# A two-block transformer kernel: a norm moved to ScalarE, two rows made by TensorE, a final norm by halves, and new instruction orders

## The reference

```
x = x + norm(attn(norm(x)))
x = x + norm(ffn(norm(x)))

attn(x):                       # g, b: gain and shift of the affine norm ln
    n  = ln(x, g, b)
    W1, W2 = mlp_h1(n), mlp_h2(n)          # 128 -> 512 -> 128, exact Gelu
    t  = ln(gelu(tril(W1 W2^T) n), g, b)
    return x + mlp_fm(ln(x + t, g, b))     # 128 -> 512 -> 128

ffn(x):                        # ternary weights, one scale per output
    h = silu(x w1 s1) * (x w2 s2)          # 128 -> 512
    h = gelu(h h1 s);  h = gelu(h h2 s)    # 512 -> 512, twice
    return h w3 s3                         # 512 -> 128
```

## Time and profile before

| | |
|---|---|
| time, median of 3 runs | 376.3 us (376.24 to 377.04) |
| profiled execution | 377.94 us |
| its span, first to last instruction | 376.1 us, mean granted TensorE clock 0.991 |
| busy, share of the span | TensorE 95%, VectorE 89%, ScalarE 79%, GpSimd 31% |
| instructions | TensorE 1751 matmuls, VectorE 978, ScalarE 515, GpSimd 186 |
| moved by transfers | 9.27 MB, most of it in the first 36 us |

### The profile page before, as it was taken

How to read it: one execution, slowest core, us unless ns; L and a number is a source line. 1 busy time by engine, 2 the same in 40 slices (tenths; PEclk the granted TensorE clock), 3 DMA queues, 4 the chain that set the end, 5 groups by cost and what they waited for, 6 DMA issues and landing times.

```text
span 376.1 us, 5883 instructions
## 1 busy us (share of the span) xinstructions
PE 358.6 (95%) x1751; PEld 289.8 (77%) x1751; DVE 333.4 (89%) x978; ACT 298.4 (79%) x515; POOL 116.8 (31%) x186
## 2 busy tenths in 40 slices
PE   7889999989999999999999999999999999999891
PEld 6658788867888788878788878788787877778681
DVE  5899999999999987999899988888978989987735
ACT  4798899787679796998688779897798769878670
POOL 5520312641182017421832083034600352061111
PEclk9899999999999999999999999999999999999998
DMA  7761000000000000100000000000000100000001
GB/s 235 227 204 57 0 2 1 3 0 0 3 0 0 2 1 0 30 0 3 0 30 0 2 15 14 0 2 29 2 2 0 30 1 0 1 27 3 0 30 31
DMA packets 8545, 9.27 MB, mean 25 GB/s; under 512 B 576, under 2 KB 6336, under 8 KB 8512
## 3 DMA queue, kind: packets, MB, share of 16 engines
q1 hardware_dynamic: 7968, 8.60, 7.5%
q10 hardware_dynamic: 544, 0.26, 0.2%
HBM read 6.77 MB, written 2.10 MB: 24 GB/s over the span
## 4 chain that ended last, share of the span: by engine, by line
PE 84%; DVE 9%; ACT 3%; issue 2%; DMA 1%; POOL 0%; POOLq 0%; SPq 0%; DVEq 0%; ACTq 0%
PE bank L1144 9%; PE bank L1142 8%; PE bank L1177 7%; PE bank L1178 7%; PE bank L1026 6%; PE bank L1030 6%; PE bank L1045 6%; PE bank L1042 6%; PE bank L1027 5%; PE bank L1043 5%; PE bank L1069 4%; PE bank L972 4%; PE bank L1125 4%; PE bank L1128 3%; PE bank L1056 3%
## 5 line engine op out<-in xcount | busy, mean ns | idle before, releaser
L434 ACT ACTIVATE h_hidden_hi<-bank,cols 128x512 fp32r<-128x512 f32 x64 | 43.1, 706 | 14.6 <-PE bank L1030 13.4
L635 DVE TENSOR_TENSOR ffn_gate_lo<-bank,ffn_gate_hi 128x512 fp32r<-128x512 f32 x64 | 42.5, 684 | 6.4 <-ACT bank L504 5.4
L635 DVE TENSOR_TENSOR h_hidden_lo<-bank,h_hidden_hi 128x512 fp32r<-128x512 f32 x64 | 42.1, 678 | 2.9 <-ACT bank L439 2.6
L504 ACT ACTIVATE bank<-bank,cols 128x512 f32<-128x512 f32 x64 | 41.4, 671 | 0.7
L439 ACT ACTIVATE bank<-bank,cols 128x512 f32<-128x512 f32 x64 | 41.4, 679 | 0.1
L1142 PE MATMUL bank<-ffn_gate_hi,ffn_w_hi 128*128 128x512 f32 x92 | 37.3, 406 | 0.8 <-ACT ffn_gate_hi L489 0.8
L1144 PE MATMUL bank<-ffn_gate_lo,ffn_w_hi 128*128 128x512 f32 x92 | 36.3, 395 | 0.4 <-DVE ffn_gate_lo L635 0.4
L301 POOL TENSOR_SCALAR ln_f_ve<-ln_f_mv 128x4 f32<-128x4 f32 x8 | 1.8, 227 | 94.9 <-DVE ln_f_mv L625 94.9
L1026 PE MATMUL bank<-aT_hi,attn_w_lo 128*128 128x512 f32 x64 | 26.6, 415 | 0.9 <-DVE attn_w_lo L635 0.6
L498 ACT ACTIVATE ffn_gate_hi<-bank,cols 128x512 fp32r<-128x512 f32 x32 | 21.5, 697 | 7.3 <-PE bank L1144 4.6
L498 ACT ACTIVATE ffn_h_hi<-bank,cols 128x512 fp32r<-128x512 f32 x32 | 21.6, 701 | 7.1 <-PE bank L1144 4.7
(11 more groups left out here) (163 smaller groups left out, 1111.5 us busy)
## 6 DMA issues: line engine op xcount, KB each, us to landing
raw<-ffn_w SPq DMA_DIRECT2D x5, 512.0 KB, 3.7
out<-X SPq DMA_DIRECT2D x7, 256.0 KB, 2.3
raw<-attn_w SPq DMA_DIRECT2D x6, 256.0 KB, 5.0
X<-x SPq DMA_DIRECT2D x2, 256.0 KB, 5.5
raw<-ffn_w SPq DMA_DIRECT2D x1, 256.0 KB, 4.0
bc<-rows SPq DMA_DIRECT2D x1, 192.0 KB, 4.1
X<-x SPq DMA_DIRECT2D x1, 128.0 KB, 2.4
X<-x ACTq DMA_DIRECT2D x1, 128.0 KB, 2.7
```

Source lines behind the costliest of these rows:

```text
L434: nc.scalar.activation(dst, bank(f"{L}u{j}", c)[:, :], ACT.Gelu, bias=bias_of(L, j)).then_inc(*hi[L].done(c, j))
L635: return nc.vector.tensor_tensor(dst, whole, high.bitcast(f32), ALU.subtract)
```

## The change

1. `y_norm(0)`, `y_norm(1)` and `y_norm(2)` leave VectorE. ScalarE gets `y_normalise(c)` for these chunks, and `y_r(c)` on GpSimd computes two more values for every chunk, -mean times r.
2. `bc` is no longer loaded. TensorE transposes the columns g and b, each broadcast over 128 columns (`make_rows`), and ScalarE copies the result to `bc` (`rows_out`). fm's second bias is loaded as one row of 512 bytes. `cols` takes the second place in SyncE's queue. `fill` makes 6 and 14 transposes instead of 26 and 3.
3. The last norm goes by halves of two tiles, each with its transposes (into two PSUM banks), statistics, aggregate, power, centring and sum.
4. `TURNS` and the orders of all five lists are new. On VectorE `gate_constants` moves from behind `attn_w_lo(1)` to the second place and `n_second(0)` from before the weight halves to behind `attn_w_lo(2)`; on ScalarE `nT_high(0)` moves from behind `attn_w_hi(1)` to behind `attn_w_hi(5)`, and `ffn_w_hi(0)` ahead of `up_hi("h1", 0, 0)`; on TensorE two `up_mm` of chunk 1 stand ahead of the scores of chunk 0.

```diff
-            sp.dma_start(bc[:, :, :], rows.rearrange("(o r) d -> o r d", o=1).broadcast_to([P, 3, D])).then_inc(rows_in, 16)
+            sp.dma_start(cols[:, :], columns).then_inc(cols_in, 16)
             attn_piece(0)
-            sp.dma_start(cols[:, :], columns).then_inc(cols_in, 16)
             attn_piece(1)
             attn_piece(2)
+            sp.dma_start(b2_row[:, :], rows[2:3, :]).then_inc(b2_in, 16)
...
             def y_r(c):
+                if c:
+                    pool.wait_ge(*y.at(c - 1))
                 rstd(y_rstd, "y", y_stats, c)
+                pool.wait_ge(*y_rstd.at(c, 1))
+                nc.gpsimd.tensor_tensor(y_mr[:, :], mv("y")[:, :, 0], LN["y"]["r"][:, :], ALU.mult).then_inc(*y_rstd.done(c, 2))
+                pool.wait_ge(*y_rstd.at(c, 2))
+                nc.gpsimd.tensor_tensor(y_shift[:, :], zeros[:, :], y_mr[:, :], ALU.subtract).then_inc(*y_rstd.done(c, 3))
...
+            def last_rstd(k):
+                pool.wait_ge(*last_ve.at(0, k))
+                half = slice(2 * k, 2 * k + 2)
+                nc.gpsimd.tensor_tensor(LN["f"]["r"][:, half], LN["f"]["ve"][:, half], neg_half[:, half], ALU.pow).then_inc(*last_r.done(0, k))
...
+            def rows_out():
+                act.wait_ge(*rows_made.at(0))
+                nc.scalar.activation(flat(bc[:, :, :]), bank("rb", 0)[:, 0:2 * P], ACT.Copy).then_inc(*rows_ready.done(0))
...
+            def y_normalise(c):
+                if c:
+                    act.wait_ge(*yT_.at(c - 1))
+                else:
+                    act.wait_ge(*ffn_lo.at(0, FP - 1))
+                act.wait_ge(*y_rstd.at(c, 3))
+                for t in range(T):
+                    last = nc.scalar.activation(YF[:, t, :], X[:, c * T + t, :], ACT.Identity,
+                                                scale=LN["y"]["r"][:, t:t + 1], bias=y_shift[:, t:t + 1])
+                last.then_inc(*y.done(c))
...
-            attn_w_hi(0); attn_w_hi(1); n_high(0); nT_high(0); attn_w_hi(2); attn_w_hi(3); up_hi("h1", 0, 0); up_hi("h1", 1, 0)
+            rows_out(); attn_w_hi(0); attn_w_hi(1); attn_w_hi(2); attn_w_hi(3); attn_w_hi(4); n_high(0); attn_w_hi(5)
+            nT_high(0); ffn_w_hi(0); up_hi("h1", 0, 0); up_hi("h1", 1, 0); up_act("h1", 0, 0); up_act("h1", 1, 0); ffn_w_hi(1)
...
-            x_st(0); x_ag(0); n_first(0); n_second(0); attn_w_lo(0); attn_w_lo(1); gate_constants(); nT_low(0); x_st(1)
+            x_st(0); gate_constants(); x_ag(0); n_first(0); attn_w_lo(0); attn_w_lo(1); attn_w_lo(2); n_second(0); attn_w_lo(3)
+            x_st(1); x_ag(1); nT_low(0); attn_w_lo(4); ffn_w_lo(0); attn_w_lo(5); up_lo("h1", 0, 0); up_lo("h1", 1, 0)
+            n_first(1); ffn_w_lo(1); up_lo("h1", 2, 0); up_lo("h1", 3, 0); n_second(1); fm_bias_add(); x_st(2)
...
+            layer_lo("b", 3, 7); last_evict_second(); last_stats(0); last_aggregate(0); last_stats(1); last_centre(0)
+            last_aggregate(1); last_sum(0); last_centre(1); last_sum(1)
...
+            def make_rows():
+
+                bank_free("rb", 0)
+                pe.wait_ge(cols_in, 16)
+                for r, col in ((R_G, C_G), (R_B, C_B)):
+                    last = nc.tensor.transpose(bank("rb", 0)[:, r * P:(r + 1) * P], cols[:, col:col + 1].broadcast_to([P, P]), ident[:, :])
+                last.then_inc(*rows_made.done(0))
...
-            fill("nT", 0, 26); n_transpose(0); fill("h1u0", 0, 3); up_mm("h1", 0, 0); up_mm("h1", 1, 0); up_mm("h1", 2, 0)
+            fill("rb", 0, 6); make_rows(); fill("nT", 0, 14); n_transpose(0); up_mm("h1", 0, 0); up_mm("h1", 1, 0)
...
+            up_mm("h1", 0, 1); up_mm("h1", 1, 1); lo_sum(2); scores(0, 0); scores(1, 0); up_mm("h2", 0, 1); up_mm("h2", 1, 1)
```

596 lines of the change are left out of this document (302 added, 294 removed), and 44 rows, old and new, of the table TURNS.

## The result

The changed kernel took 379.58 us (median of 4 runs, 379.31 to 379.71) where the kernel before took 376.27 us (375.98 to 377.04): ratio 1.0084, 95% interval 1.0066 to 1.0101. It is slower by 0.8%; 373.9 us had been forecast, and the time lies outside the range given. Its profiled execution has a span of 377.8 us, against 376.1 us. Two executions of the kernel before among those that the experiments add (403.3 and 381.9 us) were in a slower state of the chip, and are left out throughout.

A forecast was written before the change was run, and what follows sets the result against it. TensorE alone bounds the long middle, TensorE and VectorE 46.3 to 100.6 us; gains lie before 100 us and in the tail. Start -1.4, feed-forward norm -0.7, middle 0, end 0, tail -0.25: -2.35 us, giving 373.9 us, range 371.2 to 376.5 us.

The forecast's parts named there:

- rival 1: Middle: ScalarE's queue is not covered, the norm costs 2 x 1.5 us and chunk 0 gives nothing; 377.65 us, chance 0.15.
- The base: Sum: -2.35 us, worked out on the profiled execution (377.94 us), was taken off the runs' median of 376.3 us.
- step (c): Start: weights land earlier, but nT_high(0) stands behind all six pieces; third matmul at 11.6 us, 0.7 us later.
- Rival 2: Start: loads at 254, not 352 GB/s; sixth piece 1.65 us later, VectorE's lead becomes +0.2 us; 375.5 us, chance 0.10.
- step (e): Start: nine fill transposes fewer on TensorE, which ran while it waited, cost nothing and save nothing.
- (a): Start: without the bc load and with cols second in the queue, n_first(0) starts at 4.8 us, 0.55 us earlier.
- (b): Start: gate_constants ahead of GpSimd's large work saves some 1.1 us of gate_half's 1.26 us.
- Step (d): Start: the first Gelu, behind ffn_w_hi(0) on ScalarE, starts at 13.0 us; hidden, as TensorE wants it past 14.5 us.
- Feed-forward norm, -0.7 us: Chunk 0: moving the norm to ScalarE relieves VectorE by 1.0 us, partly given back by late mT; ends 0 and -2.0 us.
- Middle 0, end 0: Rest of the middle 0, from -0.5 to +1.0 us; end from 340 us 0, plus or minus 0.8 us.
- Tail, -0.25 us: Last norm by halves finishes X at 373.55 against 373.81 us, store keeps 1.9 us; ends -0.6 and +0.3 us.
- Rival 5: Second chunk's norm: n_first(1) may stall beside GpSimd's XR as gate_half did, its 1.1 us come back; 375.0 us, chance 0.09.

The follow-up runs named there:

- a0: The changed kernel once more, unedited, on the chip of the other follow-up runs: median 379.62 us.
- a_fill: The changed kernel with filler transposes in TensorE's idle time, 18 more ahead of the transposes of n and 23 behind them: median 377.98 us.
- b0: The kernel before, unedited, once more with its own profile: as fast as the kernel before; its profiled execution took 377.44 us.
- a_early_fill: a_early with filler transposes in TensorE's idle times up to 16 us: 377.84 us.
- b_rows: The kernel before with gain and shift rows made by TensorE, no broadcast load, gate constants second on VectorE: 376.01 us against 376.13 us at clock 0.993 or more.
- b_newtail: The kernel before with only the final norm done by halves: ratio 0.9993; 376.62 us against 376.44 us at clock 0.993 or more.
- b_y: The kernel before with only the feed-forward norm of chunks 0 to 2 moved to ScalarE, its shift on GpSimd: loses 5 us.
- a_early: The changed kernel with nT_high(0) behind the second weight piece on ScalarE and VectorE's low parts in the same order: executions from 376.3 to 381.1 us.
- a_ydve: The changed kernel with the feed-forward norm of chunks 0 to 2 back on VectorE: loses 3 us against the change.
- a_best: The changed kernel with a_early's order, feed-forward norm on VectorE, undivided final norm, low-half sums and flag earlier: slowest of all, branch at 47.87 us, no total given.
- b_late: The kernel before with five attention weight pieces, not two, ahead of the high part of n on ScalarE: 380.9 us, ratio 1.0087.
- b_late_fill: b_late with 35 more filler transposes between the transposes of n and the first matmul: branch at 47.06 us, no total given.

## Why the prediction was wrong

Of the 5.7 us between the forecast 373.9 us and 379.6 us, 1.6 us are the base, 1.0 us the start up to the branch, 1.7 us the stretch from there to 95 us, 0.4 us the end of TensorE's stream and 1.0 us the stores; middle and tail came as forecast. The measured time lies above every rival, rival 1 (377.65 us) included.

- **The base.** "I take the difference off the median" is the first step that failed. The sum was worked out against a profile that held a drop of the clock, told in the prediction itself (0.68 in the earlier trace rows), and was then taken off a median whose executions mostly have none. The 1.6 us between 377.94 and 376.3 us were seen and not explained.
- **Start, step (c): the third matmul at 11.6 us.** It came at 13.05 us, 13.61 us in a0, 1.4 to 2.0 us late. "The last lands at 9.7 us; its copy, `nT_high` and `aT_lo` follow one another at 0.6 us each" left out what stands in ScalarE's queue besides: it got the fourth piece at 9.00 us and then had four instructions, `n_tok_hi` among them, ahead of `aT_hi` (11.34 us). Rival 2 named a late start, but priced it without the clock, at 375.5 us. The gaps before the branch are gone as forecast: from the third matmul to the branch the change takes 31.2 us with the clock up (a_fill), the kernel before 33.7 us (b0). But with an early third matmul the change takes 34.9 us (a_early_fill, 9.64 to 44.51 us), so starting TensorE sooner buys little here. Together -1.4 us became -0.4 us against a base with a drop, and +1.7 us against b0.
- **Start, step (e): "cost nothing and save nothing".** This did not hold either. The nine fillers fewer and `n_second(0)` behind three low weight halves left TensorE idle for 1.97 us ahead of the transposes of n, and its clock fell at 9.3 us, before the 2.08 us of idleness that follow. The prediction's "some 0.25 us" for VectorE's wait became transposes of n 1.2 us later than before. No step asked what TensorE's idleness would do to its clock. Fillers in both spells gave back 1.5 us (a_fill), which is the largest single piece of the loss that a run shows; how it divides between the two spells stays open.
- **`gate_constants`, rows and first norm, (a) and (b):** right to 0.1 us (4.92 against 4.8 us, 0.15 against 0.16 us), and worth nothing by themselves: b_rows gives the third matmul 1 us and the end 0.1 us, which is within the noise; its trace has the waits for the feed-forward weights in between. Step (d), the hidden first Gelu, was right: it starts at 13.78 us and is not waited for.
- **Feed-forward norm, -0.7 us.** Each duration was right (1.67 us on ScalarE for 1.5, shift 0.2 us twice, y no sooner). The balance was not: `mT_hi`, queued behind it, starts 2.17 us after the transposes of M, where it starts 0.76 us after them in b_newtail, and the change loses 0.8 us between 84 and 95 us instead of gaining 0.7 us. TensorE's idleness before y's transposes is 0.60 us, not under 0.5 us. The prediction's "Part is given back by the late `mT`" names the likely mechanism with the wrong size; no run shows it alone.
- **Middle 0, end 0:** 0 and +0.4 us, both inside their ends. Rival 1, the norm's cost in the middle, is false for the change: ScalarE is 83% busy there and TensorE has 0.20 us of idleness in 239.40 us. It is true of b_y, where the orders were not made for the norm on ScalarE: 3.6 us at chunks 1 and 2.
- **Tail, -0.25 us:** -0.17 us. GpSimd's power of two columns takes 0.71 and 0.77 us, not 1.03 us, but VectorE's queue is what the second half waits for. Then the stores took back 1 us; "keeps its 1.9 us" was the failed step.
- **Rival 5** was right in kind and not in place: `n_first(1)` took 2.19 us instead of 1.13 us beside GpSimd's XRB, not XR. What it costs at the branch no run shows.

## What to carry to other kernels

Ask of every profiled execution how far it is from the median, and explain the difference before you take a sum off either. When a change makes TensorE wait longer at one place, price the clock as well as the wait: here idle spells of 0.6 and 1.0 us were followed by 3.4 us at half speed (b0), one of 2.0 us by 6.8 us (the change, with another 2.1 us of idleness within it), and filler transposes in the gaps were worth at least as much as the reordering of a_early, and gave steadier times. And when a trade moves work between engines whose orders are written out, a single step moved by itself (b_y, a_ydve, a_best) says little of what it is worth in the order made for it.

## What the runs showed of the hardware

- TensorE's granted clock falls to 0.50 behind idle spells and does so in some executions of one kernel and not in others: in the kernel before at 10.8 us (first profile) or at 81.4 us (b0), in b_rows at 27.7 us, in the change at 9.3 us, in a0 at 11.5 us; in all of them again in the tail. Fillers that keep it up bring the branch 1.4 to 2.2 us forward (b_late to b_late_fill, a0 to a_fill). The Trainium skill (TensorE: Matmul & The Clock Gate, Part 1) has the clock follow how busy TensorE has been; the fillers agree with it (0.50 without, 1.00 with them in the same two microseconds).
- A VectorE instruction with two operands in SBUF can wait for a GpSimd instruction beside it: `n_first(1)` took 2.19 us against 1.13 us in the kernel before, from 17.47 to 19.66 us, with XRB on GpSimd from 17.83 to 19.25 us. The whole delay is in the third of its four instructions, which took 1.40 us and not 0.34 us and ended at 19.40 us. The Trainium skill (SBUF — State Buffer, the part on the shared port pair) describes such a lock, and this trace agrees a second time.
- The same last store of 128 KB took 1.8 to 2.9 us to land in profiles of kernels whose tails differ only in order. The Trainium skill (DMA: Bandwidth & Descriptors, the anatomy of a transfer issued by GpSimd, the part on the fixed cost) puts most of a transfer's fixed cost on its completion and says that a write to HBM can make it surprisingly long; no run here shows which part of the landing grew.
- `cols`, 132 bytes for a partition, landed 2.5 us after its issue with one larger load ahead of it (2.3 to 3.1 us over the profiles), 4.0 us with two ahead (3.4 to 4.0 us).
